# Output projection at each batch's first unit, gate work one batch sooner, 128-wide maxima and gate rows, another order of first loads and tables

## The chip, the cores and the metric

The kernel runs on one core of a Trainium2 chip, as one program. The metric is the device time of one execution in microseconds; the runs of the kernel before took 355.35 us in the median of three (354.1 to 364.22). TensorE multiplies and turns tiles into PSUM banks; VectorE (DVE) and ScalarE (ACT) read PSUM; GpSimd (POOL) works on SBUF; SyncE (SP), ACT and POOL issue DMAs. Each engine runs its own list of instructions in order and waits on semaphores.

## The reference, cut to what matters

Two blocks run one after the other. Each is a residual cross-attention with a gate, and then a residual feed-forward: a top-2 mixture of eight experts with a shared one in layer 0, a token-shift channel mix in layer 1. There are 16 batches of 128 queries and 120 keys, width 128, 16 heads of 8.

```python
x = x + tanh(g_xattn[0]) * L0_xattn(layernorm(x), ctx, ctx, mask, ...)
x = x + tanh(g_ffn[0])   * L0_ffn(layernorm(x), ...)      # experts
x = x + tanh(g_xattn[1]) * L1_xattn(layernorm(x), ctx, ...)
x = x + tanh(g_ffn[1])   * L1_ffn(layernorm(x), ...)      # channel mix

# attention
attn = softmax(where(mask, -1e15, q @ k.T / sqrt(8)))
out  = (attn @ v) @ Wo + bo
# experts
scores = sigmoid(x @ gate_W) * route_scale
topk_scores, topk_idx = top_k(scores, 2)
gate_full = onehot(topk_idx) * topk_scores / topk_scores.sum()
y = sum_e gate_full[e] * (gelu(x @ W1[e] + b1[e]) @ W2[e] + b2[e])
y = y + gelu(x @ Ws1 + bs1) @ Ws2 + bs2
```

## The kernel before, in words

**Tiling.** Batches form NG = 4 groups of GB = 4; a batch has UNITS = 4 units of UH = 4 heads. Queries and keys are split into three bf16 parts (qp, kp), stored to DRAM (qparts, kparts) and loaded back stacked, so that one product over 72 rows (STACK) gives a precise score: QS and KS, two buffers by group parity, each in two halves of two batches (q_load and k_load with f = 0, 1; 3 DMAs of 192 KB or 180 KB each). Scores are formed twice. scores_q (L961 mask, L965) gives queries by keys, from which VectorE takes the negated row maxima (row_max, L443). They are split into three bf16 parts (nmp, L460 to L482), turned by TensorE (turn_max, L997, into bank 5), copied by ACT (nmT, L754) and written by POOL's DMAs into three more rows of QS (max_rows, L360). scores_k (L980 mask, L984) gives keys by queries with the maxima subtracted; ACT takes the exponential (L763, into P). values (L1013, 32-column products into bank 4) multiplies with V and a column of ones (VS, whose ones POOL writes at L365). ACT copies to cx (L770), turn_back (L1021) turns it, VectorE divides by the sum (rec L472, cn L478), turn_ctx (L1030) turns cn, ACT copies cT (L776), out_proj (L1034) multiplies with Wo into bank 5, and add_attention (L489) adds it to X.

**Order.** Each engine has its own loop over steps s = 0 to B+5 and units r = 0 to 3, written by hand. In step s TensorE does scores_q of batch s, scores_k with a lag of LAG = 10 units, values and turn_back of batch s-4, turn_ctx of batch s-5, out_proj of batch s-6, and turn_max of batch s-1 at r = 2. turn_max waits for xa_ok, the add of batch s-6, since it writes into bank 5 as well; values wait for cn_ok of the batch before, since they write into bank 4. prep spreads the projections of the next group over the steps. In layer 0 the LayerNorm, the turn and the logits (L1075) of the expert part of groups 0 to 2 run inside the attention loop. moe_top (L526 to L530) makes sigmoids and the first choice of the first eight batches, moe_gate (L538 to L560) the second choice and the gate's three bf16 parts. Both stand on VectorE behind steps B and B+1.

**Expert part.** For each group TensorE turns the gates (L1064, L1067), makes hidden products (L1052, shared expert L1054), spreads the gates over the hidden rows with a 0/1 matrix SEL (gate_rows, L1086, 24 rows), VectorE multiplies (L568), and moe_out (L1100) sums up. ACT's Gelu (L822, L826) and Exp (L805 for the logits, L763) lie in different tables; between them stands an ACT_TABLE_LOAD. The logits of the last group come in the midst of the Gelus. Layer 1's channel mix takes a Sigmoid (L838).

**Start.** SP loads X of group 0, identity, Wq and Wk, context, biases and NEG; ACT loads the rest, the mask among it, without a wait. Then SP stores kp and loads both halves of KS, and behind them the weights of layer 1 and X of groups 2 and 3 (later_loads(0)); ACT stores qp and loads both halves of QS. TensorE's first scores wait for the first halves.

## Time and profile before

| | before |
|---|---|
| median of 3 runs | 355.35 us |
| profiled execution, device time | 358.56 us |
| its span, first to last instruction | 356.6 us |
| busy: TensorE, VectorE, ScalarE, GpSimd | 286.3, 215.8, 170.8, 89.4 us |
| expert part of layer 0, about | 163 to 212 us |
| attention of layer 1, about | 212 to 320 us |

A row of the timeline gives start and duration of one instruction or of several alike (x4), and in brackets how long the engine had been idle and which instruction released it. A matmul's duration holds its latency; the next one starts before it ends, so the distance between starts is what a product costs in a full stream. Products on fp32 stand as two instructions each.

### The profile page before, as it was taken

What the parts mean: (1) busy time and instruction counts of PE and PEld (TensorE: products, weight loads), DVE (VectorE), ACT (ScalarE), POOL (GpSimd) and SP (SyncE); (2) the same over time, 40 slices, a digit from 0 to 9 for tenths busy, and PEclk for the clock granted to TensorE, in tenths of its full rate; (3) what the DMA queues carried; (4) which work ended last, traced back from release to release, by engine and by line L of the source; (5) the groups of instructions that cost most, each with busy time, mean ns of one, the idle gap of its engine ahead of it and who ended that gap; (6) DMA issues with size and microseconds to landing.
All of it is one profiled execution on the core that took longest, in us unless ns stands there. A gap on an engine that the chain in (4) does not pass through costs nothing.

```text
span 356.6 us, 7862 instructions
## 1 busy us (share of the span) xinstructions
PE 286.3 (80%) x2970; PEld 209.3 (59%) x2980; DVE 215.8 (61%) x653; ACT 170.8 (48%) x328; POOL 89.4 (25%) x154
## 2 busy tenths in 40 slices
PE   1532869999999998967999979898788878888763
PEld 0211546776777777753466458667567667666643
DVE  3530687577685684651447556867857766747672
ACT  1311226566665665544643622466557455477311
POOL 5210133323341241111001010424404333333140
PEclk9975889999999999996999999779989898699976
DMA  8267447443443230000000043445324330000021
GB/s 232 46 177 192 142 127 213 137 121 123 124 131 100 78 88 10 6 0 0 2 0 0 3 134 107 145 140 151 120 82 130 122 102 4 2 4 2 0 61 60
DMA packets 27663, 30.48 MB, mean 85 GB/s; under 512 B 13699, under 2 KB 24804, under 8 KB 26468
## 3 DMA queue, kind: packets, MB, share of 16 engines
q1 hardware_dynamic: 20366, 27.11, 25.4%
q10 hardware_dynamic: 4188, 2.47, 2.8%
q0 software_dynamic: 3072, 0.40, 0.8%
q8 instruction: 24, 0.39, 0.5%
q14 instruction: 13, 0.11, 0.1%
HBM read 22.43 MB, written 7.14 MB: 83 GB/s over the span
## 4 chain that ended last, share of the span: by engine, by line
PE 55%; DVE 15%; DMA 13%; issue 7%; ACT 5%; POOL 3%; ACTq 1%; DVEq 0%
DMA QS<-nmT 9%; PE bank L1013 6%; PE bank L984 6%; PE bank L965 6%; PE bank L1100 5%; PE bank L1052 4%; PE bank L961 3%; PE bank L1021 3%; PE bank L980 3%; DMA QS<-qparts 3%; DVE nmx L443 2%; PE bank L922 2%; PE bank L930 2%; DVE xn L434 2%; PE bank L1034 2%
## 5 line engine op out<-in xcount | busy, mean ns | idle before, releaser
L443 DVE TENSOR_REDUCE nmx<-bank 128x4 f32<-128x480 f32 x128 | 81.5, 652 | 43.9 <-PE bank L965 43.5
L763 ACT ACTIVATE P<-bank 120x512 f32<-120x512 f32 x128 | 76.2, 598 | 34.3 <-PE bank L984 32.5
L360 POOL DMA_DIRECT2D QS<-nmT x96 | 47.4, 498 | 144.9 <-ACT nmT L754 144.5
L984 PE MATMUL bank<-QS,KS 75*120 75x128 bf16 x512 | 54.2, 232 | 5.1 <-DMA QS<-nmT 4.7
L965 PE MATMUL bank<-KS,QS 72*128 72x120 bf16 x512 | 52.2, 228 | 3.6 <-DVE nmx L443 2.4
L984 PEld LDWEIGHTS bank<-QS,KS 75*120 75x120 bf16 x512 | 47.1, 143 | 13.5 <-issue 6.0
L965 PEld LDWEIGHTS bank<-KS,QS 72*128 72x128 bf16 x512 | 40.7, 104 | 22.6 <-issue 10.6
L1013 PE MATMUL bank<-P,VS 120*32 120x128 f32 x1024 | 38.4, 296 | 6.1 <-DVE cn L478 4.2
L961 PE MATMUL bank<-MB,IDH 128*128 128x480 bf16 x64 | 24.9, 389 | 13.2 <-DMA QS<-qparts 9.7
L1013 PEld LDWEIGHTS bank<-P,VS 120*32 120x32 f32 x1024 | 29.4, 118 | 9.6 <-ACT P L763 6.6
L434 DVE TENSOR_SCALAR xn<-X,mv,rstd 128x128 f32<-128x128 f32 x64 | 23.0, 479 | 13.6 <-POOL rstd L330 13.6
L489 DVE SCALAR_TENSOR_TENSOR X<-bank,TG,X 128x128 f32<-128x128 f32 x32 | 11.0, 345 | 32.6 <-PE bank L1034 32.5
L328 POOL TENSOR_TENSOR ve<-mv,epsT 128x4 f32<-128x4 f32 x16 | 3.2, 197 | 101.0 <-DVE mv L420 101.0
L770 ACT ACTIVATE cx<-bank 128x512 f32<-128x512 f32 x32 | 19.1, 596 | 18.2 <-PE bank L1013 18.2
L741 ACT ACTIVATE kp<-bank,BC 128x480 bf16<-128x480 f32 x16 | 10.6, 660 | 35.4 <-PE bank L910 16.9
L980 PE MATMUL bank<-IDH,MB 128*120 128x512 bf16 x64 | 25.7, 401 | 1.6 <-DMA QS<-nmT 1.5
L1021 PE MATMUL bank<-IDF,cx 128*128 128x128 f32 x128 | 20.1, 280 | 0.4 <-ACT cx L770 0.3
L568 DVE TENSOR_TENSOR FF<-bank,FF 128x512 f32<-128x512 f32 x16 | 10.7, 689 | 14.3 <-PE bank L1086 14.3
L1052 PE MATMUL bank<-XT,WT 128*128 128x512 f32 x32 | 18.9, 686 | 0.2 <-ACT FF L822 0.2
L754 ACT ACTIVATE nmT<-bank 48x128 bf16<-48x128 bf16 x32 | 8.6, 268 | 20.6 <-PE bank L997 20.6
L910 PE MATMUL bank<-CT,WT 128*128 128x480 f32 x16 | 9.9, 708 | 9.7 <-DMA NEG<-in_negidh 7.5
L922 PE MATMUL bank<-IDF,xn 128*128 128x128 f32 x64 | 12.4, 328 | 6.2 <-DVE xn L434 6.1
(115 smaller groups left out, 446.6 us busy)
## 6 DMA issues: line engine op xcount, KB each, us to landing
KS<-kparts SPq DMA_DIRECT2D x48, 180.0 KB
QS<-qparts SPq DMA_DIRECT2D x42, 192.0 KB
kparts<-kp SPq DMA_DIRECT2D x24, 120.0 KB, 2.1
qparts<-qp SPq DMA_DIRECT2D x21, 128.0 KB, 3.0
QS<-nmT POOLq DMA_DIRECT2D x96, 4.0 KB, 2.3
QS<-qparts ACTq DMA_DIRECT2D x6, 192.0 KB
out<-X SPq DMA_DIRECT2D x4, 256.0 KB, 2.3
X<-in_x SPq DMA_DIRECT2D x3, 256.0 KB, 14.2
```

Of the source, the lines that this page charges most:

```text
L360: po.dma_start(QS[G % 2][STACK + p:STACK + p + 1, k // 2, :, (k % 2) * S:(k % 2 + 1) * S], nmT[Bi % 2][p * H:(p + 1) * H, :]).then_inc(m_l ...
L434: ins = nc.vector.tensor_scalar(xn[:, i, :], X[:, GB * g + i, :], mv[:, i, 0:1], rstd[:, i:i + 1], ALU.subtract, ALU.mult)
L443: ins = nc.vector.tensor_reduce(nmx[Bi % 2][:, UH * r:UH * r + UH], bank[U % 2][:, 0:UH * SK].rearrange("p (h k) -> p h k", k=SK), AX.X, A ...
L763: nc.scalar.activation(P[Bi % 2][:, hh, :], src, ACT.Exp, scale=SCALE).then_inc(exp_done, 1)
L922: last = nc.tensor.transpose(o[:, i * S:(i + 1) * S], xn[:, i, :], IDF[:, :])
L961: mm(o[:, 0:UH * SK].rearrange("p (h k) -> p h k", k=SK), IDH[:, :], MB[:, b, :].unsqueeze(1).broadcast_to([S, UH, SK]), start=True, stop= ...
L965: last = mm(o[:, j * SK:(j + 1) * SK], QS[G % 2][0:STACK, k // 2, h, (k % 2) * S:(k % 2 + 1) * S], KS[G % 2][0:STACK, k // 2, h, (k % 2) * ...
L980: mm(o[0:SK, :].rearrange("p (h s) -> p h s", s=S), MB[:, b, :], IDH[:, :].unsqueeze(1).broadcast_to([S, UH, S]), start=True, stop=False, ...
L984: last = mm(o[0:SK, j * S:(j + 1) * S], KS[G % 2][0:ROWS, k // 2, h, (k % 2) * SK:(k % 2 + 1) * SK], QS[G % 2][0:ROWS, k // 2, h, (k % 2) ...
L1013: last = mm(bank[4][VW * j:VW * (j + 1), r * S:(r + 1) * S], VS[G % 3][:, k, h, :], P[Bi % 2][:, h, :], start=True, stop=True, skip_group_ ...
L1021: last = nc.tensor.transpose(bank[4][:, r * S:(r + 1) * S], cx[Bi % 2][:, r * S:(r + 1) * S], IDF[:, :])
L1052: mm(bank[j % 2][:, :], W(W1 + k), XT4[:, g, :], start=True, stop=True).then_inc(h_done, 1)
```

## The change

It has six parts. (1) out_proj of batch s-6 stands behind scores_q of the first unit, ahead of turn_max and scores_k, and no longer behind scores_k of the second. (2) moe_top(0, 8) runs at the end of step B-1 and moe_gate(0, 8) in step B at r = 1, ahead of the normalisation in that step. (3) nmp is 128 columns wide with zeros behind 48, and turn_max writes 128 rows; SEL and gpT have 128 rows with zeros behind 24; the shared expert's hidden product is 128 wide. (4) ACT only negates the last group's logits, and POOL raises e to them. (5) Exp is loaded ahead of layer 1 behind the last Gelu, and Sigmoid in layer 1 behind the last exponential, each by a small activation. (6) ACT's first loads wait for X of group 0, POOL's fill of VS waits for the first LayerNorm, SP's second half of KS waits for the first half of QS; POOL has five more memsets, and SP's load of SEL and TensorE's loop wait for all of them.

```diff
@@ sync
             k_store(0)
             k_load(0, 0)
+            sp.wait_ge(q_ld[0][0], 16 * PARTS)
             k_load(0, 1)
...
                 if i == 3:
+                    sp.wait_ge(pool_c, 13)
@@ gpsimd
             ln_rstd_(ln_no(0, 0))
+            po.wait_ge(xn_ok, 1)
             for i in range(3):
                 po.memset(VS[i][:, :, :, HD:VW], 1.0).then_inc(pool_c, 1)
+            for i in range(2):
+                po.memset(nmp[i][:, PARTS * H:], 0.0).then_inc(pool_c, 1)
+            po.memset(gpT[:, :], 0.0).then_inc(pool_c, 1)
+            po.memset(SEL[:, :], 0.0).then_inc(pool_c, 1)
+            po.memset(eT[:, :, :], math.e).then_inc(pool_c, 1)
...
                 if L == 0:
+                    po.wait_ge(lg_neg, 1)
+                    po.wait_ge(lg_evac, NG - 1)
+                    c = sc[:, GB * (NG - 1):B, :]
+                    po.tensor_tensor(c, eT[:, :, :], c, ALU.pow).then_inc(lg_evac, 1)
                     ln_rstd_(ln_no(2, 0))
@@ vector
                             add_attention(L * B + s - 6)
+                        if L == 0 and s == B and r == 1:
+                            moe_gate(0, B // 2)
                         if r == 3 and 4 <= s < B + 4:
                             parts_and_normalise(None, L * B + s - 4)
...
-                    if L == 0 and s == B:
+                    if L == 0 and s == B - 1:
                         moe_top(0, B // 2)
-                    if L == 0 and s == B + 1:
-                        moe_gate(0, B // 2)
@@ scalar
             nc.scalar.activation(warm[:, :], epsT[:, :], ACT.Exp)
+            a.wait_ge(x_in[0], 16)
...
                 a.wait_ge(lg_done, g + 1)
...
+                if g == NG - 1:
+                    nc.scalar.activation(sc[:, GB * g:GB * g + GB, :], QB[:, 0:GB * E].rearrange("p (b e) -> p b e", e=E),
+                                         ACT.Copy, scale=-1.0).then_inc(lg_neg, 1)
+                    return
...
+                        if L == 1 and U == B * UNITS:
+                            nc.scalar.activation(warm[:, :], epsT[:, :], ACT.Sigmoid)
...
+                        if g == NG - 1:
+                            nc.scalar.activation(warm[:, :], epsT[:, :], ACT.Exp)
@@ tensor
-                nc.tensor.transpose(bank[5][:, :].bitcast(BF16)[0:PARTS * H, 0:S],
-                                    nmp[Bi % 2][:, :, :].rearrange("p c h -> p (c h)"), IDH[:, :]).then_inc(nt_done, 1)
+                nc.tensor.transpose(bank[5][:, :].bitcast(BF16)[:, 0:S], nmp[Bi % 2][:, :], IDH[:, :]).then_inc(nt_done, 1)
...
-                    mm(bank[j % 2][0:HID, :], W(WSH, HID), XT4[:, g, :], start=True, stop=True).then_inc(h_done, 1)
+                    mm(bank[j % 2][:, :], W(WSH), XT4[:, g, :], start=True, stop=True).then_inc(h_done, 1)
...
                             scores_q(L * B + s, r)
+                        if r == 0 and 6 <= s:
+                            out_proj(L * B + s - 6)
                         if r == (2 if s > 1 else 0) and 1 <= s < B + 1:
                             turn_max(L * B + s - 1)
...
-                        if r == 1 and 6 <= s:
-                            out_proj(L * B + s - 6)
```

TensorE, a step of layer 0 from the first unit's scores to the second's. Before, the projection (bank<-WT,cT) stands behind two score products of both kinds and the values:

```order
L965 MATMUL bank<-KS,QS 128x120 x4
L980 MATMUL bank<-IDH,MB 120x512 [waits exp_done]
L984 MATMUL bank<-QS,KS 120x128 x4
L1013 MATMUL bank<-P,VS 32x128 [waits cn_ok,exp_done]
L1013 MATMUL bank<-P,VS 32x128 x15
L961 MATMUL bank<-MB,IDH 128x480 [waits max_done]
L965 MATMUL bank<-KS,QS 128x120 x4
L980 MATMUL bank<-IDH,MB 120x512 [waits exp_done]
L984 MATMUL bank<-QS,KS 120x128 x4
L1034 MATMUL bank<-WT,cT 128x128 [waits ct_evac]
```

Of the changed kernel, at the same place (its line 1056 is out_proj, 1003 and 1007 are scores_k, 1035 the values):

```order
L988 MATMUL bank<-KS,QS 128x120 x4
L1056 MATMUL bank<-WT,cT 128x128 [waits ct_evac]
L1003 MATMUL bank<-IDH,MB 120x512 [waits exp_done]
L1007 MATMUL bank<-QS,KS 120x128 x4
L1035 MATMUL bank<-P,VS 32x128 [waits cn_ok,exp_done]
L1035 MATMUL bank<-P,VS 32x128 x15
L984 MATMUL bank<-MB,IDH 128x480 [waits max_done]
L988 MATMUL bank<-KS,QS 128x120 x4
L1003 MATMUL bank<-IDH,MB 120x512 [waits exp_done]
L1007 MATMUL bank<-QS,KS 120x128 x4
```

The projection has moved ahead of the first scores_k, the values and the second unit, and with it its wait for ct_evac.

VectorE, behind the last row maxima of layer 0, where L482 is the last part of the maxima of batch 15. Before, an add and a normalisation come first, and moe_top begins with the row of sc:

```order
L482 TENSOR_TENSOR nmp<-nmr,nmp 128x16 [waits dve_c]
L489 SCALAR_TENSOR_TENSOR X<-bank,TG,X 128x128 [waits op_done]
L472 RECIPROCAL rec<-bank 128x16 [waits ct_done,cn_ok,cb_done]
L478 TENSOR_TENSOR cn<-bank,rec 128x128 [waits dve_c]
L526 TENSOR_SCALAR sc<-sc 128x64 [waits w_in2,lg_evac]
L527 RECIPROCAL sc<-sc 128x64 [waits dve_c]
```

Of the changed kernel, the end of moe_top, the add of batch 10 and the start of moe_gate, and then the end of moe_gate with the normalisation of batch 12 behind it:

```order
L555 TENSOR_REDUCE mw<-eq 128x8 [waits dve_c]
L556 TENSOR_TENSOR oh<-eq,mw 128x64 [waits dve_c]
L544 SCALAR_TENSOR_TENSOR s<-oh,sc 128x64 [waits dve_c]
L503 SCALAR_TENSOR_TENSOR X<-bank,TG,X 128x128 [waits op_done,dve_c]
L552 TENSOR_REDUCE m<-s 128x8 [waits pool_c]
L553 TENSOR_TENSOR eq<-s,m 128x64 [waits dve_c]
```

and, with the rows of moe_gate between left out,

```order
L572 TENSOR_TENSOR gr<-gx,gp 128x64 [waits dve_c]
L573 CAST gp<-gr 128x8x8 [waits dve_c]
L574 TENSOR_TENSOR gp<-gr,gp 128x8x8 [waits dve_c]
L486 RECIPROCAL rec<-bank 128x16 [waits ct_done,cn_ok,cb_done]
L492 TENSOR_TENSOR cn<-bank,rec 128x128 [waits dve_c]
L503 SCALAR_TENSOR_TENSOR X<-bank,TG,X 128x128 [waits op_done]
```

The nine instructions of moe_top and sixteen of moe_gate now stand ahead of the normalisation (rec, cn), one add between them.

SP, at the first stacked loads of the changed kernel; before, the same rows stand there without the wait for q_ld00:

```order
L269 DMA KS<-kparts 24x1x3840 [waits k_st]
L269 DMA KS<-kparts 24x1x3840 x2
L269 DMA KS<-kparts 24x1x3840 [waits k_st,q_ld00]
L269 DMA KS<-kparts 24x1x3840 x2
L238 DMA WT<-in_wts 128x512
L224 DMA X<-in_x 128x4x128 x2
```

The second half of KS, the weights of layer 1 and X of groups 2 and 3 stand behind that wait.

## Rows read from the trace of the kernel before

**Rows 1.** The waits of TensorE over the whole span: us in total, times, longest

```profile
PE bank L961 <- DMA QS<-qparts: 9.7, 1, 9.7
...
PE bank L997 <- DVE X L489: 5.2, 11, 1.1
...
PE bank L1013 <- DVE cn L478: 4.2, 8, 0.7
```

**Rows 2.** The timeline, first 36 us: start, duration, engine, line, tiles, [idle before <- releaser]

```profile
6.93 4.02 POOL L365 MEMSET VS<- 120x1536 f32 x3
7.02 4.58 DVE L434 TENSOR_SCALAR xn<-X,mv,rstd 128x128 f32<-128x128 f32 x4 [1.42 <-POOL rstd L330]
...
11.65 1.11 PE L922 MATMUL bank<-IDF,xn 128*128 128x128 f32 x4 [2.17 <-DVE xn L434]
...
21.20 1.11 DVE L434 TENSOR_SCALAR xn<-X,mv,rstd 128x128 f32<-128x128 f32 x4 [1.41 <-POOL rstd L330]
21.55 4.23 ACTq L715 DMA_DIRECT2D QS<-qparts  x6
...
33.28 0.58 PE L961 MATMUL bank<-MB,IDH 128*128 128x480 bf16 x1 [9.73 <-DMA QS<-qparts]
```

**Rows 3.** DMA queues, 24 to 26 us: packets, MB, share (q10 is ACT's)

```profile
q10 hardware_dynamic: 28, 0.20, 30.6%
```

**Rows 4.** The timeline of one step of layer 0

```profile
119.59 0.38 PE L980 MATMUL bank<-IDH,MB 128*120 128x512 bf16 x1
...
119.76 0.27 ACT L776 ACTIVATE cT<-bank 128x128 f32<-128x128 f32 x1
```

**Rows 5.** The timeline of one step of layer 1

```profile
294.29 0.39 PE L984 MATMUL bank<-QS,KS 75*120 75x128 bf16 x4
...
294.66 0.27 ACT L776 ACTIVATE cT<-bank 128x128 f32<-128x128 f32 x1
...
295.23 1.08 PE L1013 MATMUL bank<-P,VS 120*32 120x128 f32 x16 [0.55 <-DVE cn L478]
```

**Rows 6.** The timeline in the expert layer

```profile
199.54 1.02 PE L930 MATMUL bank<-xnT,WT 128*128 128x512 f32 x2
...
200.50 0.38 PE L1086 MATMUL bank<-gpT,SEL 24*128 24x512 bf16 x1
...
200.81 1.13 PE L1052 MATMUL bank<-XT,WT 128*128 128x512 f32 x2
```

**Rows 7.** The chain that ended last: start, duration, what

```profile
88.22 0.86 PE bank L930 x2
```

**Rows 8.** The timeline at the end of layer 0's attention

```profile
140.62 0.17 DVE L482 TENSOR_TENSOR nmp<-nmr,nmp 128x16 bf16<-128x16 f32 x1
...
142.66 0.22 PE L997 MATMUL bank<-IDH,nmp 128*48 128x128 bf16 x1 [0.54 <-DVE X L489]
...
144.44 0.18 DVE L526 TENSOR_SCALAR sc<-sc 128x64 f32<-128x64 f32 x1
...
144.83 1.08 PE L1013 MATMUL bank<-P,VS 120*32 120x128 f32 x32
...
146.83 0.23 DVE L530 SCALAR_TENSOR_TENSOR s<-oh,sc 128x64 f32<-128x64 f32 x1
...
148.56 0.21 DVE L538 TENSOR_REDUCE m<-s 128x8 f32<-128x64 f32 x1
...
152.17 0.22 DVE L560 TENSOR_TENSOR gp<-gr,gp 128x64 bf16<-128x64 f32 x1
```

**Rows 9.** Groups by shape: busy us, mean ns | idle before

```profile
L330 POOL TENSOR_TENSOR rstd<-ve,powT 128x4 f32<-128x4 f32 x16 | 16.4, 1024 | 1.3
...
L338 POOL TENSOR_TENSOR X<-X,tgbo 128x512 f32<-128x512 f32 x8 | 10.2, 1277 | 2.6 <-DVE tgbo L498 2.5
...
L822 ACT ACT_TABLE_LOAD x2 | 2.6, 1283 | 4.3 <-DVE FF L568 4.3
```

**Rows 10.** Span and mean granted clock of the core

```profile
core 0: 356.6 us, clock 0.909
```

More of the change, by code:

```diff
@@ L38 @@
 from contextlib import ExitStack
+import math
 F32 = mybir.dt.float32
@@ L87, in gated_blocks @@
         NEG = sb("NEG", [128, 128], BF16)
-        SEL = sb("SEL", [PARTS * E, NBLK * 128], BF16)
+        SEL = sb("SEL", [128, NBLK * 128], BF16)
+        eT = sb("eT", [S, GB, E])
         RANK = sb("RANK", [128, B, E])
@@ L111, in gated_blocks @@
         nmr = sb("nmr", [S, H])
-        nmp = [sb(f"nmp{i}", [S, PARTS, H], BF16) for i in range(2)]
+        nmp = [sb(f"nmp{i}", [S, 128], BF16) for i in range(2)]
         nmT = [sb(f"nmT{i}", [PARTS * H, S], BF16) for i in range(2)]
@@ L136, in gated_blocks @@
         gx = sb("gx", [S, B, HID + E + 1])
-        gpT = sb("gpT", [PARTS * E, GT], BF16)
+        gpT = sb("gpT", [128, GT], BF16)
         xsh = sb("xsh", [D, B, S + 1])
@@ L176, in gated_blocks @@
         op_done = sem("op_done"); xa_ok = sem("xa_ok")
-        lg_done = sem("lg_done"); lg_evac = sem("lg_evac"); g_ok = sem("g_ok"); gt_done = sem("gt_done"); gt_evac = sem("gt_evac")
+        lg_neg = sem("lg_neg"); lg_done = sem("lg_done"); lg_evac = sem("lg_evac"); g_ok = sem("g_ok"); gt_done = sem("gt_done"); gt_evac = sem("gt_evac")
         h_done = sem("h_done"); h_act = sem("h_act"); gb_done = sem("gb_done"); hs_ok = sem("hs_ok")
@@ L243, in later_loads @@
                 if i == 3:
+                    sp.wait_ge(pool_c, 13)
                     sp.dma_start(W2S[:, :], w2sh).then_inc(w_in2, 16)
-                    sp.dma_start(SEL[:, :], sel).then_inc(w_in2, 16)
+                    sp.dma_start(SEL[0:PARTS * E, :], sel).then_inc(w_in2, 16)
                     sp.dma_start(RANK[:, :, :], rank).then_inc(w_in2, 16)
@@ L459, in parts_and_normalise @@
                         v.wait_ge(nt_done, Bi - 1)
-                    first = mark(nc.vector.tensor_copy(nmp[i][:, 0, :], nmx[i][:, :]))
+                    first = mark(nc.vector.tensor_copy(nmp[i][:, 0 * H:1 * H], nmx[i][:, :]))
                 if c:
@@ L469, in parts_and_normalise @@
                     v.wait_ge(dve_c, first)
-                    second = mark(nc.vector.tensor_tensor(nmr[:, :], nmx[i][:, :], nmp[i][:, 0, :], ALU.subtract))
+                    second = mark(nc.vector.tensor_tensor(nmr[:, :], nmx[i][:, :], nmp[i][:, 0 * H:1 * H], ALU.subtract))
                 if c:
@@ L474, in parts_and_normalise @@
                     v.wait_ge(dve_c, second)
-                    third = mark(nc.vector.tensor_copy(nmp[i][:, 1, :], nmr[:, :]))
+                    third = mark(nc.vector.tensor_copy(nmp[i][:, 1 * H:2 * H], nmr[:, :]))
                 if c:
@@ L481, in parts_and_normalise @@
                     v.wait_ge(dve_c, third)
-                    nc.vector.tensor_tensor(nmp[i][:, 2, :], nmr[:, :], nmp[i][:, 1, :], ALU.subtract).then_inc(nm_ok, 1)
+                    nc.vector.tensor_tensor(nmp[i][:, 2 * H:3 * H], nmr[:, :], nmp[i][:, 1 * H:2 * H], ALU.subtract).then_inc(nm_ok, 1)
             def add_attention(Bi):
@@ L804, in logit_exp @@
                 a.wait_ge(lg_done, g + 1)
-                nc.scalar.activation(sc[:, GB * g:GB * g + GB, :], (KVB if g < NG - 1 else QB)[:, 0:GB * E].rearrange("p (b e) -> p b e", e=E),
+                if g == NG - 1:
+                    nc.scalar.activation(sc[:, GB * g:GB * g + GB, :], QB[:, 0:GB * E].rearrange("p (b e) -> p b e", e=E),
+                                         ACT.Copy, scale=-1.0).then_inc(lg_neg, 1)
+                    return
+                nc.scalar.activation(sc[:, GB * g:GB * g + GB, :], KVB[:, 0:GB * E].rearrange("p (b e) -> p b e", e=E),
                                      ACT.Exp, scale=-1.0).then_inc(lg_evac, 1)
@@ L809, in gt_copy @@
                 a.wait_ge(gt_done, g + 1)
-                nc.scalar.activation(gpT[:, :], bank[5][:, :].bitcast(BF16)[0:PARTS * E, 512:1024], ACT.Copy)
+                nc.scalar.activation(gpT[0:PARTS * E, :], bank[5][:, :].bitcast(BF16)[0:PARTS * E, 512:1024], ACT.Copy)
                 if g >= 2:
@@ L1141, in _ @@
             pe.wait_ge(c_in2, 16)
-            pe.wait_ge(pool_c, 8)
+            pe.wait_ge(pool_c, 13)
             pe.wait_ge(mb_ok, 1)
```

## The prediction

> **What bounds the kernel now.** I read four views, in this order: the waits of TensorE over the whole span, the timeline of the first 34 us with what the DMA queues moved in it, the timelines of one attention step in each layer and of the end of layer 0, and the costs by shape. The waits [rows 1] say that TensorE stands still for one long reason, 9.7 us at the start for the first stacked queries, and then for many short ones: 5.2 us in 11 pieces for VectorE's residual add (L489) ahead of the turn of the maxima (L997), and 4.2 us in 8 pieces for the normalised context (L478) ahead of the values (L1013). Between them it is busy, so the attention loops are bound by TensorE's own stream, at the end of each layer by a chain of latencies, and at the start by loads. I go through the edits in the order of the program.
>
> **Start.** VectorE takes 4.58 us over four normalisations while POOL fills VS for 4.02 us at the same time; the same four take 1.11 us later, with POOL silent [rows 2]. TensorE waits 2.17 us for them [rows 2]. The memsets now wait for xn_ok, so this wait goes: -2.1. POOL's new memsets come behind and are small (gpT and SEL 128x512, by the rate of VS, 4.02 us for 4608 elements a row, about 0.5 us each if bf16 is no faster); all are over near 14 us, and TensorE first asks for them after 21 us. Then the first q_load: SP has issued six KS loads ahead, ACT issues the QS loads from 21.55 us, and TensorE gets the first half at 33.28 us [rows 2]. Each half of QS is 3 x 192 KB = 0.58 MB. In the stretch 24 to 26 us ACT's queue moves 0.20 MB [rows 3]; to land at 33.28 it must have been slower after that, when KS second half, weights and X flow through SP's. The changed SP holds all of that back until the first QS half has landed. At 0.10 MB in a us (the rate of 24 to 26 us, still shared) 0.58 MB take 5.8 us. The issue comes 2.1 us sooner, at 19.45; with some 2 us from issue to flow (21.55 against 24) that gives 27.2, and at 1.5 times the rate 25.3. I take 26.5: 6.8 us before 33.28, of which 2.1 are the first item. Bounds: 4 (no faster queue, only the 2.1 and a little) and 8.5. What is late next: KS second half, the layer-1 weights that the bias product waits for, X of group 2; batch 2 needs KS some 12 us behind the start, so I take these as hidden. ACT's loads start at 4.3 us instead of 0.9, and end about when its first copy is due; cost 0 to 0.5.
>
> **Output projection one place earlier.** Layer 0: TensorE is through with the first scores of a step and moves on at 119.59, cT is copied from 119.76 to 120.03 [rows 4]. The projection now stands there, so TensorE waits 0.44 + 0.05 for the semaphore = 0.5 us. Layer 1, without mask products: on at 294.29, cT until 294.93 [rows 5], 0.7 us. There are ten such steps in each layer (6 to 15): 5 + 7 = +12.0. Behind the waiting projection stand the transposed scores of the unit, the exponentials on ACT, and the values. Given back: add_attention no longer holds VectorE until unit 1, so the turn of the maxima need not wait for it: 5.2 us of [rows 1]. And in layer 1 the values arrive later than the normalised context (cT at 294.98, projection and scores 0.5, so 295.5 against 295.23 [rows 5]), so the wait for cn is swallowed: of 4.2, some 3.5 lie in these steps. Net 12.0 - 5.2 - 3.5 = +3.3. So this edit by itself costs rather than gains. Bounds -1 and +7.
>
> **128-wide shapes.** In the expert part the two halves of a projection last from 199.54 to the selection product at 200.50, 0.96 us [rows 6]; the same pair ahead of a 128-row product takes 0.86 [rows 7]. The selection product (512 columns) holds the array until 200.81, 0.31 us [rows 6]; 512 columns at 2.4 GHz are 0.21. So about 0.1 us is lost on each side of the 24-row product. The Trainium skill, TensorEngine Tiling (Array Packing), Key Properties, says that a change of tiling mode drains the array; the rows agree in that there is a gap on both sides, and give its size. 13 selection products and 4 halves of the 64-column shared expert stand in a stretch that TensorE bounds: 17 x 0.19 = 3.2. The 48-column turn of the maxima occurs 32 times; its gaps I take at 0.15, for 4.8. An eighth of it lies under other waits: -7.0 together. The 32-column values and 24-column turn of gates keep their shapes, so those drains stay. Bounds 0 (the gap comes from elsewhere) and -8.
>
> **Gate work one batch sooner.** moe_top takes 144.44 to 147.06 = 2.6 us of VectorE, moe_gate 148.56 to 152.39 = 3.8 us [rows 8]. Both now stand ahead of work that TensorE waits for. moe_top begins when the last maxima are done (140.79) and ends at 143.4, the add of batch 10 behind it at 143.8, and the turn of the last maxima starts at 143.9 instead of 142.66. moe_gate then runs until 147.7, ahead of the normalisation of batch 12, which is ready at 148.3; the values of batch 13 want it and ran at 144.83 [rows 8]: 3.5 us late. Later in the drain moe_gate is gone from its old place, where it held the add of batch 12 and the next LayerNorm, and this gives back 0.6. +2.9. Bounds 0 (if the drain has more slack than I see) and +4. The gate rows themselves were not waited for.
>
> **Last group's exponential on POOL.** ACT loses two table loads of 1.28 us each [rows 9], which TensorE hardly waits for: -0.3. In exchange POOL computes a power of 128x32. The nearest row is a power of 128x4, 1.02 us; an add of 128x512 takes 1.28 us [rows 9]. If the time beyond some 0.2 of start goes with the elements, 32 take 0.2 + 8 x 0.83 = 6.8 us; if it is fixed, 1.0. moe_top of the second half waits for it and comes 5.5 us later at the high end (6.8 less the table load that stood there), the gating of the next hidden products waits behind it on VectorE, which has between 3 and 4 us to spare there by my estimate, and TensorE stalls 2 us. I take the high end, since the add shows that elements cost little only where the operation is simple: +2.0. The Trainium skill, GPSIMD Engine Reference, on the per-element model, gives about 2.6 cycles per element for a two-input operation; the add agrees (2.5 ns per element), and if power followed it the 2.0 would be 0. No run here shows which.
>
> **Tables ahead of need.** Exp ahead of layer 1 saves at most 1.28; TensorE waits little there: -0.4. Sigmoid ahead of k_relu is loaded in ACT's idle time, but the projection of batch 13 now waits for a cT that ACT copies behind k_relu and r_sig: I take +0.7 for layer 1's drain in all.
>
> **Sum.** -6.8 + 3.3 - 7.0 + 2.9 - 0.3 + 2.0 - 0.4 + 0.7 = -5.6 us. The profiled execution took 358.56 us (span 356.6 and 2.0 around it), so its like takes 353.0. The median of the runs is 355.35, 3.2 below the profiled one, and the forecast for the median is 355.35 - 5.6 = 349.8 us. About 2% (7.1 us) is what a measurement of this kernel can tell from no change.
>
> **Rivals.**
> - *As summed*, 346.5 to 353: 0.42.
> - *Power and gates hidden.* POOL's power is as cheap as its add, and the drain of layer 0 has slack for moe_gate. For it: TensorE waits in the drain on three engines in turn, so a delay of one may lie under another. Against: 147.7 is three us beyond 144.83 [rows 8]. 349.8 - 2.0 - 2.9 = 345: 0.22.
> - *The shapes do nothing.* The 0.1 us gaps come from the change of operands and not from the tile. Against: the pair of [rows 7] goes over to other operands too, and shows none. 349.8 + 7 = 357: 0.12.
> - *The start is only moved.* KS second half, 0.54 MB, and the weights are issued 5 us later and land while rows of maxima and the next group are in flight; batch 2 waits. For it: SP's queue is in order. It gives back what was won beyond the first 2.1: 349.8 + 4.7 = 354.5: 0.13.
> - *Slower: the clock falls.* The new pauses of 0.5 to 0.7 us come in every step. The mean granted clock is 0.909 [rows 10], so 18% of the time is at 1.2 GHz and the rest at 2.4. Work that TensorE bounds takes twice as long at the low level; 26 us more of it there would cost 13 us: 349.8 + 13 = 363. It decides from 12.7 us (25 us more at the low clock) on, 40% more than the 64 us now, and I see no row for that much: 0.08.
> The rest, 0.03, is for mishaps of several kinds. Range for 8 in 10: 342 to 357.5, which takes in the first four. Faster by over 2% (below 348.2): the second rival and some 0.4 of the first, 0.39; slower 0.09; within 2% 0.52.
>
> **What would show it.** Right: TensorE's first masked scores at 26 to 27 us; new waits of TensorE at the projection for cT of 10 us and more in some 20 pieces, the waits of the turn for the add gone, no or few waits of the values for cn in layer 1; the selection product with its pair 0.2 us shorter; values of batch 13 some 3 us behind the turn_back that they now follow, with moe_gate in front; POOL's power at 7 us and moe_top behind it. Wrong: a power of 1 us, no wait for cT, first scores still beyond 30 us, or more stretches at the low clock.

## The result: slower, and outside the range

| | before | changed |
|---|---|---|
| median of the runs | 356.15 us (4 runs) | 361.82 us (4 runs, 360.75 to 365.72) |
| ratio | | 1.018, 95% interval 1.010 to 1.026 |
| profiled execution, device time | 358.56 us | 360.75 us |
| its span | 356.6 us | 358.8 us |
| busy: TensorE, VectorE, ScalarE, GpSimd | 286.3, 215.8, 170.8, 89.4 us | 280.5, 213.0, 167.0, 95.9 us |

I had said 349.8, between 342 and 357.5. The changed kernel is 5.7 us slower. Ratios, here and below, compare those runs of each kernel that lie within about 1.5% of its fastest, so they can differ from a quotient of the medians. In the profiled executions TensorE is busy 5.8 us less and the span is 2.2 us longer, so waits have come in. The two executions differ in the granted clock too, 0.909 before and 0.937 changed, which shortens the busy time of the second. In the rows of the changed kernel line numbers are 22 or 23 higher for TensorE's products in the attention (L997 is now L1020, L1013 is L1035, L1034 is L1056).

The waits of TensorE, us in total, times, longest:

```profile
PE bank L1056 <- ACT cT L791: 18.4, 30, 2.3
PE bank L984 <- DMA QS<-qparts: 7.2, 1, 7.2
...
PE bank L937 <- ACT kp L756: 4.0, 2, 3.7
...
PE bank L1020 <- DVE X L503: 3.2, 3, 1.1
...
PE bank L984 <- issue: 2.7, 1, 2.7
...
PE bank L1035 <- DVE cn L492: 1.5, 2, 0.8
```

Before, the same view has for the projection:

```profile
PE bank L1034 <- ACT cT L776: 3.3, 3, 1.3
```

So 15.1 us of the projection's wait for cT are new, and it is now the largest of all; against [rows 1] the waits for the add and for cn have shrunk by 2.0 and 2.7. Grown as well are the wait for ACT's first kp copy, from 0.3 to 4.0 us, and one of 2.7 us, before 0.2, that no shown event ends.

The start, by the timeline of the changed kernel:

```profile
4.34 5.87 ACTq L711 DMA_DIRECT2D X<-in_x  x1
...
6.14 1.11 DVE L448 TENSOR_SCALAR xn<-X,mv,rstd 128x128 f32<-128x128 f32 x4 [1.42 <-POOL rstd L334]
...
7.31 4.01 POOL L370 MEMSET VS<- 120x1536 f32 x3 [1.21 <-DVE xn L448]
...
12.62 0.66 ACT L756 ACTIVATE kp<-bank,BC 128x480 bf16<-128x480 f32 x1 [10.38 <-issue]
...
24.45 4.49 ACTq L730 DMA_DIRECT2D QS<-qparts  x6
...
31.72 2.56 SPq L269 DMA_DIRECT2D KS<-kparts  x3
...
31.75 0.58 PE L984 MATMUL bank<-MB,IDH 128*128 128x480 bf16 x1 [7.20 <-DMA QS<-qparts]
```

The normalisations do take 1.11 us, as forecast, in place of the 4.58 of [rows 2]. But ACT, which now begins its loads at 3.4 us, is held 5.87 us by the issue of X for group 1, and its first copy comes at 12.62, behind the last of these issues. QS is issued at 24.45, later than the 21.55 of [rows 2], and the first scores come at 31.75, only 1.5 us sooner than the 33.28 of before.

One step of layer 0, one of layer 1, and the end of layer 0:

```profile
122.10 0.27 ACT L791 ACTIVATE cT<-bank 128x128 f32<-128x128 f32 x1
...
122.42 0.49 PE L1056 MATMUL bank<-WT,cT 128*128 128x128 f32 x2 [0.33 <-ACT cT L791]
...
301.22 0.27 ACT L791 ACTIVATE cT<-bank 128x128 f32<-128x128 f32 x1
...
301.54 0.49 PE L1056 MATMUL bank<-WT,cT 128*128 128x128 f32 x2 [0.53 <-ACT cT L791]
...
164.74 1.28 ACT L841 ACT_TABLE_LOAD   x1
166.03 0.69 ACT L841 ACTIVATE FF<-bank,BC 128x512 f32<-128x512 f32 x1
166.62 0.27 ACT L791 ACTIVATE cT<-bank 128x128 f32<-128x128 f32 x1
...
166.94 0.80 PE L1056 MATMUL bank<-WT,cT 128*128 128x128 f32 x2 [2.29 <-ACT cT L791]
```

In a step the wait is 0.33 and 0.53 us, where I had taken 0.5 and 0.7 from [rows 4] and [rows 5]. In the drain (the steps s = 16 to 21, in which a layer has no scores_q left) it is up to 2.29: ACT has a table load and a gelu queued ahead of the copy. Before, TensorE waited 1.29 us at the same projection. The drains' waits were not in my sum for the projection.

### The profile page after: what moved, and what is told of

Same layout as the page of the kernel before. It is cut to its first block, busy times and chain, and to the rows that moved or that the text cites. A ratio compares the mean times of both kernels' runs of the same rounds, so it can differ in the third digit from the quotient of the medians.

```text
span 358.8 us, 7867 instructions
## 1 busy us (share of the span) xinstructions
PE 280.5 (78%) x2967; PEld 208.8 (58%) x2980; DVE 213.0 (59%) x653; ACT 167.0 (47%) x328; POOL 95.9 (27%) x160
## 4 chain that ended last, share of the span: by engine, by line
PE 49%; DVE 16%; DMA 10%; issue 10%; ACT 6%; POOL 5%; ACTq 3%; DVEq 0%; another core or an unknown queue 0%; POOLq 0%
PE bank L1035 7%; DMA QS<-nmT 7%; PE bank L1007 5%; PE bank L988 5%; PE bank L1074 4%; PE bank L1043 3%; PE bank L1056 3%; PE bank L984 3%; PE bank L1003 3%; DVE nmx L457 3%; PE bank L953 2%; PE bank L1122 2%; POOL rstd L334 2%; ACTq L711 2%; ACT cT L791 2%
## 5 line engine op out<-in xcount | busy, mean ns | idle before, releaser
L1007 PE MATMUL bank<-QS,KS 75*120 75x128 bf16 x512 | 52.5, 228 | 2.9 <-DMA QS<-nmT 2.8
L988 PEld LDWEIGHTS bank<-KS,QS 72*128 72x128 bf16 x512 | 39.4, 103 | 23.6 <-issue 10.2
L1007 PEld LDWEIGHTS bank<-QS,KS 75*120 75x120 bf16 x512 | 47.1, 141 | 10.2 <-issue 2.6
L1035 PE MATMUL bank<-P,VS 120*32 120x128 f32 x1024 | 37.1, 289 | 1.5 <-DVE cn L492 1.5
L984 PE MATMUL bank<-MB,IDH 128*128 128x480 bf16 x64 | 24.7, 386 | 13.2 <-DMA QS<-qparts 7.2
L1056 PE MATMUL bank<-WT,cT 128*128 128x128 f32 x64 | 16.0, 334 | 18.4 <-ACT cT L791 18.4
L1035 PEld LDWEIGHTS bank<-P,VS 120*32 120x32 f32 x1024 | 27.9, 115 | 4.2 <-ACT P L778 1.7
L448 DVE TENSOR_SCALAR xn<-X,mv,rstd 128x128 f32<-128x128 f32 x64 | 19.3, 364 | 12.5 <-POOL rstd L334 12.5
L1056 PEld LDWEIGHTS bank<-WT,cT 128*128 128x128 f32 x64 | 10.0, 196 | 24.3 <-ACT cT L791 23.8
L841 ACT ACTIVATE FF<-bank,BC 128x512 f32<-128x512 f32 x16 | 10.8, 687 | 14.7 <-DVE FF L582 9.2
L933 PE MATMUL bank<-CT,WT 128*128 128x480 f32 x16 | 10.9, 770 | 8.2 <-DMA NEG<-in_negidh 6.8
L1122 PE MATMUL bank<-WT,FF 128*128 128x128 f32 x128 | 17.0, 275 | 0.0
```

Of the source, the lines that this page charges most:

```text
L984: mm(o[:, 0:UH * SK].rearrange("p (h k) -> p h k", k=SK), IDH[:, :], MB[:, b, :].unsqueeze(1).broadcast_to([S, UH, SK]), start=True, stop= ...
L988: last = mm(o[:, j * SK:(j + 1) * SK], QS[G % 2][0:STACK, k // 2, h, (k % 2) * S:(k % 2 + 1) * S], KS[G % 2][0:STACK, k // 2, h, (k % 2) * ...
L1007: last = mm(o[0:SK, j * S:(j + 1) * S], KS[G % 2][0:ROWS, k // 2, h, (k % 2) * SK:(k % 2 + 1) * SK], QS[G % 2][0:ROWS, k // 2, h, (k % 2) ...
L1035: last = mm(bank[4][VW * j:VW * (j + 1), r * S:(r + 1) * S], VS[G % 3][:, k, h, :], P[Bi % 2][:, h, :], start=True, stop=True, skip_group_ ...
L1056: mm(bank[5][:, 0:128], cT[Bi % 2][:, :], W(WO[Bi // B]), start=True, stop=True).then_inc(op_done, 1)
L1122: last = mm(bank[4][:, i * D:(i + 1) * D], lhs, rhs, start=(k == 0), stop=(k == NBLK))
```

## The experiments

Every kernel was compared with the kernel before on the same chip; medians of before lay between 358.3 and 359.8 us. Ratios are to before, with 95% intervals. Parts have letters: O projection, W 128-wide shapes, G gate work, P power on POOL, T table preloads, and of the start M (memsets wait for xn), Q (SP waits for the first half of QS), A (ACT's loads wait for X).

| kernel | parts | ratio | interval |
|---|---|---|---|
| e1_outproj | O | 1.0306 | 1.0233 to 1.0379 |
| e10_out_layer1 | O, layer 1 only | 1.0236 | 1.0160 to 1.0312 |
| e2_shapes | W | 0.9858 | 0.9792 to 0.9925 |
| e3_start | M Q A | 0.9787 | 0.9732 to 0.9842 |
| e6_memset | M | 0.9845 | 0.9776 to 0.9914 |
| e8_memset_queue | M Q | 0.9843 | 0.9729 to 0.9957 |
| e9_act_loads | A | 1.0002 | 0.9943 to 1.0062 |
| e4_gates | G | 1.0083 | 1.0034 to 1.0133 |
| e5_tables | P T | 0.994 | 0.9859 to 1.002 |
| c1_shapes_start | W M Q A | 0.9831 | 0.9728 to 0.9933 |
| e16_shapes_memset_queue | W M Q | 0.9741 | 0.9682 to 0.9799 |
| c3_best | W M Q T | 0.9635 | 0.9535 to 0.9734 |
| e12_best_act | W M Q T A | 0.9865 | 0.9796 to 0.9935 |
| e13_best_gates | W M Q T G | 0.9871 | 0.9801 to 0.9941 |
| e14_best_pow | W M Q T P | 0.9812 | 0.9721 to 0.9904 |
| e15_best_out | W M Q T O | 0.9933 | 0.9875 to 0.9991 |
| e7_undo_out | all but O | 0.9992 | 0.9928 to 1.0056 |
| e11_changed_early_loads | all but A | 1.0027 | 0.9971 to 1.0083 |

**The projection (e1, e10, e7, e15).**

```diff
                             scores_q(L * B + s, r)
+                        if r == 0 and 6 <= s:
+                            out_proj(L * B + s - 6)
...
-                        if r == 1 and 6 <= s:
-                            out_proj(L * B + s - 6)
```

> The kernel before with one edit: the output projection stands at the first unit of a step instead of the second. Theory (the projection's wait for cT is the dear part of the change): the changed kernel shows 18.4 us of waits for cT in 30 pieces, drains included; given back are the 5.2 us of waits of the turn for the residual add and about 3 of the 4.2 us for cn; so 6 to 10 us slower, values of the batches from 2 on later by about 0.4 to 0.7 us a step. Rival 1 (the forecast's own sum): +3.3 us. Rival 2 (the waits only move within a step, since the step is bound by TensorE's stream in either order): within 1 us, and the starts of values as before.

> The kernel before with the output projection at the first unit in layer 1 alone. By the forecast's terms, 7.0 new less 3.5 of cn and half of the 5.2 of the add: +1 us. Theory from the trace with both layers moved (values of batch 12 later by 4.8 than those of batch 0, those of batch 31 by 5.4 than those of batch 16, and 3 us more at the seam and in the drain): 5 to 7 us slower, about half of 11. Rival: the clock makes the rest, the layers don't add up, below 3 us or above 9.

> The changed kernel with the output projection put back at the second unit of a step, all else as changed. Theory (the projection is the bulk of the loss and adds up with the rest): 10 to 12 us faster than the changed kernel, so about 0.985 of the kernel before. Rival (with the other parts in place the projection's waits replace others, and cost less than alone): 4 to 7 us faster, so 1.00 of the kernel before.

> The best kernel so far (shapes, memset, queue, table preloads) with the output projection at the first unit of a step. Theory (its price is the same in any company, 8 to 11 us): waits for cT near 18 us in 30 pieces, ratio 0.99 to 1.00 if the best kernel is 0.965 on this chip too. Rival (in this company it is cheaper, as the step has shorter products to wait behind): 0.98 to 0.985.

Alone it costs 11.0 us (8.4 to 13.6), more than either theory or rival of e1 said; in layer 1 alone 8.5 (5.7 to 11.2), again above what I expected; added to the best kernel 3% (0.9635 to 0.9933), as the theory of e15 had it; in the whole change 1.9%, 6.7 us (0.9992 to 1.018), which is the rival of e7 and not my theory. It loses in every company. Waits of TensorE in e1:

```profile
PE bank L1034 <- ACT cT L776: 18.7, 30, 2.3
...
PE bank L997 <- DVE X L489: 0.7, 1, 0.7
...
PE bank L1013 <- DVE cn L478: 0.7, 1, 0.7
```

and the same row in e10, where layer 1 alone has the new order:

```profile
PE bank L1034 <- ACT cT L776: 12.2, 16, 1.9
```

One of the 16 pieces in e10 is layer 0's old one of 1.29 us, so layer 1 has 10.9 in 15. By their starts, the 18.7 us of e1 are 8.6 in 15 pieces in layer 0 and 10.2 in 15 in layer 1; 3.3 in 3 were there before, all in the drains. I counted ten steps a layer, but the projection also runs in the six steps of each drain. In the changed kernel the twenty steps that I counted hold 9.2 of the 18.4 us (0.36 and 0.57 a step, where I had 0.5 and 0.7, 12.0 in all), and the two drains hold the other 9.2.

What the order costs in the changed kernel is seen against e7, which has all else:

```profile
PE bank L1020 <- DVE X L503: 6.4, 11, 1.7
PE bank L1035 <- DVE cn L492: 6.3, 9, 2.1
...
PE bank L1056 <- ACT cT L791: 2.4, 2, 1.3
```

16.0 us of waits for cT come in; 3.2 of the add, 4.8 of cn and smaller ones for the exponentials and the maxima's rows go. TensorE's idle time, span less busy time, rises from 72.0 to 78.3 us, 6.3, at nearly the same granted clock (0.928 and 0.937), and the time by 6.7 (some 3 to 10). There the waits account for the price.

In e1 they don't: 15.4 us come in, 4.5 of the add and 3.5 of cn go, with smaller ones idle time rises by 1.6 only, from 70.3 to 71.9, and it is TensorE's busy time that is 13.2 us longer. Part of this is the clock: in layer 1's loop, 246 to 324 us, e1's trace has a granted clock of 0.77, before 0.89 from 236 to 310. The rest is open, and with it why the order is dearer alone. One thing differs in the loop of layer 0: from the values of batch 4 to those of 12 it is 57.6 us in e1 and 54.5 to 55.9 in the other kernels without W, 0.2 to 0.4 us a step; with W it is 55.8 in e15, e11 and the changed kernel and 53.8 to 55.1 in all but one of those with W and without O, some 0.2 us a step against my 0.24.

**The start (e3, e6, e9, e8, e12, e11).** The three added waits, from above, are Q, M and A.

```diff
             k_load(0, 0)
+            sp.wait_ge(q_ld[0][0], 16 * PARTS)
             k_load(0, 1)
...
             ln_rstd_(ln_no(0, 0))
+            po.wait_ge(xn_ok, 1)
...
             nc.scalar.activation(warm[:, :], epsT[:, :], ACT.Exp)
+            a.wait_ge(x_in[0], 16)
```

> The kernel before with the three edits of the start: VS memsets behind the first normalisation, ACT's first loads behind X of group 0, SP's second half of KS behind the first half of QS. Theory (the start gain is spent again): first masked scores 1 to 2 us sooner than 33.28, but SP's queue runs 2.5 us later for group 1, so TensorE stands still for batch 4's first scores; the time comes out 0 to 2 us slower than before. Rival (the forecast): 6.8 us faster. Second rival: first scores' 1.5 us stay as a gain, 1 to 2 us faster.

> The kernel before with one edit of the start: the VS memsets stand behind the first normalisation. Theory (forecast): the four normalisations take 1.1 instead of 4.6 us, TensorE's wait of 2.2 us for them goes, first scores 2 us sooner, 2.1 us faster. Rival: ACT's copies or the DMA queues are next, less than 0.7 us. By the forecast the other two edits of the start then hold what is left of the 7.6 us that the three gave together.

> The kernel before with one edit of the start: ACT's first loads wait for X of group 0. Theory: the issue of X of group 1 holds ACT for some 5 us in place of 2.3, its first copy comes at 12 to 13 us instead of 9.6, kparts are stored at 16.5 to 17.5 all the same, since the slow normalisation is late by as much; first scores as before or up to 1 us later, time within 1 us. Rival (the forecast's 0 to 0.5 us also where the normalisation is fast): the edit is harmless in any company, and then the memset and queue edits without it give the first scores at 30 as with it.

> The kernel before with two of the three edits of the start: VS memsets behind the first normalisation, and SP's second half of KS behind the first half of QS; ACT's first loads stay where they were. Theory (ACT's later loads cost what the memset edit gains): the memset edit alone stored kparts at 13.2 us and issued QS from 18.2; with the queue edit alone the first half of QS takes 6.5 to 7.3 us from issue to the first scores where it took 11.1 to 11.9; both together bring the first scores to 25 to 27 us, what the forecast said. Of this some 4 us are lost again behind it, at the layer's bias weights and at batch 4's first scores, where SP's queue is late. Rival: first scores stay at 30, since ACT's loads never mattered. In time: theory 6 to 8 us faster than before (ratio 0.978 to 0.985), rival as the memset edit alone (0.985 to 0.99).

> The best kernel so far (shapes, memset, queue, table preloads; 0.9635 of before) with ACT's first loads behind X of group 0 added. Theory: kparts stored at 16.5 instead of 13.2, first scores at 30 to 31 instead of 26.2, and the stall at batch 4 grows from 1.6 to between 2.6 and 3.7 us with the half clock behind it; ratio 0.974 to 0.982. Rival (as alone): no effect, 0.96 to 0.968.

> The changed kernel without one edit: ACT's first loads are issued at once again instead of behind X of group 0. Theory (this edit undoes the memset edit's gain, and I had put it at 0 to 0.5): first scores at 26 to 27 instead of 31.75, 3.5 to 5 us faster than the changed kernel, ratio to before 1.004 to 1.010. Rival: the later steps are bound by the projection's waits and SP's queue in either case, less than 1.5 us, ratio 1.015.

In e3 the forecast won in time and my theory after the result fell: the three together are worth 2.1%, 7.6 us. It did not win by its own path, since the first scores come at 30.29 and not at 26.5. The traces sort the edits cleanly by when the first masked scores start: without M and Q at 33.15 to 36.33 us (seven kernels, before and e9 among them), with M at 30.05, with M and Q at 26.20 to 27.21 (seven), with M, Q and A at 30.29 to 31.75 (five). What I forecast, 26.5, holds where A is left out. The spread of 3 us without M and Q, among kernels whose start is nearly the same, says that 33.28 was an early one: M brings 3.1 to 6.3 us at this place. The best kernel and then the same with A:

```profile
7.00 1.12 DVE L441 TENSOR_SCALAR xn<-X,mv,rstd 128x128 f32<-128x128 f32 x4 [1.42 <-POOL rstd L332]
...
9.59 0.66 ACT L748 ACTIVATE kp<-bank,BC 128x480 bf16<-128x480 f32 x1 [7.35 <-PE bank L921]
...
13.21 1.43 SPq L256 DMA_DIRECT2D kparts<-kp  x3
...
18.26 4.65 ACTq L722 DMA_DIRECT2D QS<-qparts  x6
...
26.21 0.58 PE L972 MATMUL bank<-MB,IDH 128*128 128x480 bf16 x1 [5.87 <-DMA QS<-qparts]
```

```profile
4.47 5.55 ACTq L704 DMA_DIRECT2D X<-in_x  x1
...
12.43 0.66 ACT L749 ACTIVATE kp<-bank,BC 128x480 bf16<-128x480 f32 x1 [10.20 <-issue]
...
16.96 1.43 SPq L256 DMA_DIRECT2D kparts<-kp  x3
...
30.58 0.58 PE L973 MATMUL bank<-MB,IDH 128*128 128x480 bf16 x1 [6.24 <-DMA QS<-qparts]
```

A moves ACT's first copy from 9.59 to 12.43, the store of kparts by 3.7 us, the issue of QS from 18.26 to 24.16, and the first scores by 4.4 us. With the old slow normalisation it does nothing (e9, 1.000), because that was late by as much; M lifts that cover. In time A costs 2.3% on the best kernel (more than e12 said; its pause before batch 4 is 1.7 us and did not grow as I had said) and 1.5%, 5.5 us (2.0 to 9.0), on the whole change, a little more than e11's theory. But two other pairs say less: e16 to c1 0.9%, and e8 to e3 even 0.6% the other way, within the noise. So the delay of the first scores is shown in every pair, and its price in time only roughly.

Q works nearly as forecast: from issue to the first scores it is 11.9 us in e6 and 8.0 in c3_best, and in the changed kernel ACT's queue alone moves in 26 to 32 us what before shared the engines with SP's. The two answers of the queue view, before and changed:

```profile
q1 hardware_dynamic: 681, 0.87, 61.0%
q10 hardware_dynamic: 62, 0.39, 23.6%
```

```profile
q10 hardware_dynamic: 141, 0.90, 51.0%
```

ACT's queue moves 0.90 MB in place of 0.39 in the six us. But part of it is paid back. In the changed kernel SP issues group 1's QS at 50.81 us, before at 48.49; TensorE stands from 54.81 to 57.46 before batch 4's first scores, and then runs at half the clock, 1.2 GHz, (windows of the changed kernel: busy times with counts, then granted clock, DMA share, GB/s):

```profile
54.00:56.00 2.00, 0.81 (x9) 0.51 (x6) 1.86 (x7) 1.18 (x2) 1.12 (x3) 1.00 0.48 151
56.00:58.00 2.00, 0.54 (x5) 0.46 (x6) 0.00 (x1) 0.00 (x0) 0.00 (x0) 0.93 0.54 164
58.00:60.00 2.00, 2.00 (x28) 1.61 (x29) 0.66 (x1) 0.60 (x1) 0.00 (x0) 0.50 0.87 228
60.00:62.00 2.00, 2.00 (x31) 1.19 (x23) 0.19 (x1) 0.61 (x2) 0.00 (x0) 0.72 1.00 261
```

The same pause is 1.2 to 3.7 us long in the twelve kernels with Q, and in before there is none at batch 4. No row names what ends it in the changed kernel; that it is the late loads of group 1 is read from the order of issue. A like pause for the row maxima stands some batches ahead in both kernels (2.85 us up to 48.12 before, 2.86 up to 46.29 changed), and behind it too the granted clock is 0.50, from 50 to 52 and from 48 to 50 us. The pause at batch 4 would explain why e8 (M and Q, 0.9843) is not measurably better than e6 (M, 0.9845).

**The shapes (e2, c1, e16).**

```diff
-        SEL = sb("SEL", [PARTS * E, NBLK * 128], BF16)
+        SEL = sb("SEL", [128, NBLK * 128], BF16)
...
-                    mm(bank[j % 2][0:HID, :], W(WSH, HID), XT4[:, g, :], start=True, stop=True).then_inc(h_done, 1)
+                    mm(bank[j % 2][:, :], W(WSH), XT4[:, g, :], start=True, stop=True).then_inc(h_done, 1)
```

> The kernel before with the 128-wide shapes alone (turn of the maxima, selection product, shared expert's hidden rows, and the memsets that pad them, behind the VS memsets). Theory: as forecast, each 24- or 48-row product loses about 0.1 us on either side; 5 to 7 us faster, and the product behind the turn of the maxima starts 0.06 us after it where TensorE runs on, instead of 0.17. Rival: the gap comes from the change of operands, or the saving lies under the waits for other engines; less than 2 us either way.

> The kernel before with the two parts that paid alone, 128-wide shapes and the start edits. Theory (they lie in different stretches and add up): -5.1 and -7.6 give 12.7 us, ratio 0.964 to 0.968, faster than both kernels. Rival (faster steps run into the later loads of SP's queue for group 1 and the gain of the start is given back at batch 4): ratio 0.975 to 0.985.

> The best kernel so far without the two table preloads. Theory: the preloads are worth 0.4 to 2 us, so 0.968 to 0.975. Rival (0.9635 was partly the luck of the clock in layer 1, 0.98 there where others have 0.87 to 0.94): 0.975 to 0.985, with the best kernel's true place nearer to 0.975.

Alone they give 1.4%, 5.1 us (2.7 to 7.5). The selection products, before and in the best kernel:

```profile
170.68 0.38 PE L1086 MATMUL bank<-gpT,SEL 24*128 24x512 bf16 x1
172.06 0.39 PE L1086 MATMUL bank<-gpT,SEL 24*128 24x512 bf16 x1
```

```profile
175.34 0.38 PE L1096 MATMUL bank<-gpT,SEL 128*128 128x512 bf16 x1
176.41 0.38 PE L1096 MATMUL bank<-gpT,SEL 128*128 128x512 bf16 x1
```

A period of 1.38 us becomes 1.07: 0.30 saved on each where TensorE runs through, more than my 0.19. Elsewhere some of it is lost again, I take it where VectorE is waited for: from the first selection product to the last it is 41.8 us in all eight kernels with neither W nor P and 39.4 in the six with W and without P whose records are whole, so 2.4 saved of 3.2 forecast. The turn of the maxima gives little by itself. The next product started 0.17 us behind it in the median, and starts 0.13 behind it with W, 0.04 to 0.05 us a step, not 0.15. Where the projection has moved too it starts 0.17 behind it in e1 and 0.06 in e15, e11 and the changed kernel, so in the order of the changed kernel the wide turn saves 0.11 a step. Why the order matters here no run shows. In c1 shapes and start together give 1.7%, not 3.5, as the rival had it: its trace has the longest of the pauses before batch 4, 3.7 us. e16 and c3_best without A come to 2.6% and 3.7%, as expected.

**The gates (e4, e13).**

```diff
+                        if L == 0 and s == B and r == 1:
+                            moe_gate(0, B // 2)
...
-                    if L == 0 and s == B:
+                    if L == 0 and s == B - 1:
                         moe_top(0, B // 2)
-                    if L == 0 and s == B + 1:
-                        moe_gate(0, B // 2)
```

> The kernel before with moe_top and moe_gate of the first half one place sooner. Theory (VectorE's gate work now stands ahead of the normalisation of batches 12 and 13): values of batch 13 start 2 to 3 us later than at 144.83, half a us is won back in the drain, 2 to 3 us slower. Rival (the drain of layer 0 has slack): 0 to 0.5 us.

> The best kernel so far with the gate work of the first half one place sooner. Theory: as alone, values of batch 13 some 3 us later, a ratio 0.008 above 0.9635. Rival: the faster drain leaves VectorE less slack, 0.015 above.

+3.0 us alone (1.2 to 4.8). The step from batch 12's values to 13's grows from 4.65 to 7.91 in e4, and 1.0 comes back by batch 15. In e13 the trace shows the same 3.3 and 1.0; the ratio is 2.4% above c3_best's, which is the rival's and not the theory's size, and 1.3% above e16's; the intervals of all three do not decide more. In the changed kernel the gate work ends right ahead of the normalisation that the values wait for:

```profile
149.71 0.23 DVE L574 TENSOR_TENSOR gp<-gr,gp 128x64 bf16<-128x64 f32 x1
150.14 0.29 DVE L492 TENSOR_TENSOR cn<-bank,rec 128x128 f32<-128x128 f32 x1
...
150.58 1.08 PE L1035 MATMUL bank<-P,VS 120*32 120x128 f32 x32 [0.83 <-DVE cn L492]
```

**Power and tables (e5, e14).**

```diff
+                    c = sc[:, GB * (NG - 1):B, :]
+                    po.tensor_tensor(c, eT[:, :, :], c, ALU.pow).then_inc(lg_evac, 1)
```

> The kernel before with the table edits alone: the last group's exponential as a power on POOL, Exp loaded ahead of layer 1, Sigmoid loaded ahead of k_relu. The four parts measured so far give, in us of a time of 359.8: projection +11.0, shapes -5.1, start -7.6, gates +3.0, together +1.3, and the whole change is +6.4 (1.018 of 356). Theory A (parts add up): what is missing, about +5, sits here: the power of 128x32 takes 5.4 us and moe_top of the second half waits for it, TensorE stands still in the expert part, and the drain of layer 1 is later; 4 to 6 us slower. Theory B (parts don't add up: the start gain is eaten where the projection waits anyway): this part is worth the forecast's +2.0 or less.

> The best kernel so far with the last group's exponential as a power on POOL. Theory: the power takes 5.4 us, VectorE's top-k waits for it and the expert part of TensorE stands still once for 1.6 us and once for 1.0: 2 to 3 us, a ratio 0.006 to 0.009 above 0.9635. Rival 1: it is hidden, 0.000 to 0.002. Rival 2: the rest of the missing 3.5% sits here, 0.015 or more above.

Together they are within the noise (0.994), so nothing is missing here; theory A of e5 fell. The power takes the same time in every kernel that has it, in the changed one:

```profile
L397 POOL TENSOR_TENSOR sc<-eT,sc 128x32 f32<-128x32 f32 x1 | 5.4, 5427 | 10.6 <-ACT sc L821 10.6
```

5.43 us against 1.02 for 128x4 [rows 9] is 0.16 us an element of a row above the first four. The Trainium skill, GPSIMD Engine Reference, on the per-element model, gives about 2.6 cycles per element for a two-input operation, as a floor; by its 1.2 GHz that is 2.2 ns, an estimate. The add of [rows 9] is near it with 2.5 ns an element; the power takes some 60 times that. With W the stretch of the selection products grows from 39.38 to 40.83 in e14, so 1.5 us are not hidden (forecast 2.0); in e5, without W, it grows from 41.80 to 44.79, 3.0 us. In time e14 is 1.8% above c3_best, as its second rival had it, and 0.7% above e16; these do not decide more.

**The best kernel.**

> The kernel before with the parts that paid: 128-wide shapes, memset and queue edits of the start, Exp and Sigmoid tables ahead of need; projection, gate work, ACT's loads and the last group's exponential as before. Theory: first scores at 25 to 27 us, the start is worth 6 to 8 us, shapes 4 to 5, tables 1: ratio 0.965 to 0.975. Rival (seen with shapes and start together, 0.983 with a stall of 3.7 us at batch 4 and the half clock behind it): the faster loop runs into SP's late loads and the half clock, ratio 0.98 to 0.99.

345.34 us in the median of six (341.61 to 350.23) against 358.63 of before on its chip: it beats both kernels. Three of the five kernels made from it (e12, e13, e14) came out above what their theories counted from 0.9635, and the fit below puts it 1.1% higher, so its true place is probably somewhat above that. Without the two preloads, on another chip, it was 0.9741; the intervals overlap, and e5 has the preloads only together with the power, so whether they are worth the difference is open.

**Do the parts add up?** Those alone sum to 0.997 and the change is 1.018, which puzzled me. One price for each part, fitted to all nineteen ratios by least squares, misses none by more than 1.3 times half its interval: O +2.15% (layer 0 -0.2, layer 1 +2.4), G +1.1, A +0.6, P +0.15, T +0.1, W -0.6, Q -0.5, M -1.55, each uncertain by 0.4 to 0.9. They sum to +1.4% for the change. The split of O by layers rests on e10 alone and that of M from Q on e6 alone, and the traces do not bear the first out: the new waits for cT are 7.3 us in layer 0 and 8.2 in layer 1 (e1). Within these uncertainties the ratios need no interaction. The traces show two all the same: A with M at the start, and O with W in the turn of the maxima. W at 2 us and not 5 is what the fit prefers, and I can't settle between them.

## Why the prediction was wrong, point by point

Two steps failed: the count of the projection's waits, and ACT's later loads put at almost nothing. Each was taken back by itself out of the changed kernel (e7, e11), and each time the kernel came back to the time of before.

- **Projection, +3.3, measured 6.7 in the change and 11.0 alone: the first step that failed.** "There are ten such steps in each layer" left out the six steps of each drain. They hold 9.2 us of the 18.4 us of waits, 6.8 more than in e7. The steps that were counted hold 9.2 and not 12.0, so the number came nearer by an error the other way. The 8.7 given back had the right size: 8.0 in e1 and in the change. The drain of layer 1 had +0.7 under another item and that of layer 0 nothing, though ACT's table load and gelus stand ahead of the copy there. The bound of +7 does not hold the price alone.
- **ACT's loads, "cost 0 to 0.5": the second step that failed.** They cost 4.4 us at the first scores on the best kernel and 4.5 in the change, where leaving them as they were brought 5.5 us. The reason given, that they "end about when its first copy is due", held only for issues at their old length; the issue of X took 5.87 us and not 2.33.
- **Start, -6.8, the rest of it.** With A left out the place is right (first scores 26.2 to 27.2 where 26.5 was said). M was sized too small: the issue of QS comes 3.3 us sooner than in before, not 2.1, and in time it is 5.6 us (3.1 to 8.0). Q has 3.9 where 4.7 was said. That the total fits is in part luck. That "KS second half, the layer-1 weights, X of group 2" are hidden failed too, as far as the order of issue tells: the pause before batch 4 is the rival "the start is only moved", in part.
- **128-wide shapes, -7.0, measured -5.1 alone, -2.1 by the fit.** The selection products were nearly right (2.4 of 3.2). The turn of the maxima was carried over from the one shape to the other without a row: 0.04 us a step in the old order, and 0.11 in the new, for 0.15.
- **Gate work, +2.9: right**, +3.0 alone and 3.3 less 1.0 in the trace.
- **Power, +2.0: right in kind** (7 us forecast, 5.43 measured; 1.5 not hidden). **Tables: nothing measurable**, as said.
- **The rival of the clock.** In the four runs of the changed kernel the mean clock was 0.927, in the 102 of before 0.928: it did not fall. With O alone it was 0.891, and 0.912, 0.910 and 0.902 in e10, e11 and e15; but e6 and e8, without O, have 0.908 and 0.907. Within runs of before, 0.01 of mean clock goes with 1.45 us, so in e1 some 5 us of 13.8 (means over all its runs) may be the clock's; that is a correlation, not shown as a cause.

With the prices of the fit (7.7, -2.1, -5.2 with A, 3.9, 0.7) the sum is +5.0 instead of -5.6; the change took +5.7. The fit has the changed kernel among its nineteen, so this says only that no single part is hidden.

## What to carry to other kernels

Count a moved instruction through its loop's prologue and drain, not only its steady steps, and look in each at what its producer's engine has queued ahead. Where one edit takes away a delay, ask what other delay was hidden behind it, and price every further edit against the shortened chain: one that is free alone can eat the whole gain. Holding a queue back for the first load works, but what it held back must still be in time for the next group.
